# The last feed-forward layer of a four-layer model: one-hot tiles of 128 columns, additions between gathers, dense matmuls ahead of each search

## What is computed

```
logits = xf @ Wr + br                      # xf: 2048 x 128, 8 experts
Sm = softmax(logits, axis=-1)
G_t, idx_t = top_k(Sm.T, 256)              # per expert: its 256 tokens
G = G_t.T
idx = idx_t.T
tokens = xf[idx]
group = arange(8) // 2                     # two experts share W_up
mid = silu(einsum('keh,ehf->kef', tokens, W_up[group]) + b_up[group])
out = einsum('kef,efh->keh', mid, W_down) + b_down
y = zeros_like(xf).at[idx].add(G[..., None] * out)

x = x + tanh(g_ffn[3]) * y                 # with xf = layernorm(x)
```

## Time and profile before

| | us |
|---|---|
| median of 3 runs | 2270.3 |
| their lowest and highest | 2265.45, 2286.44 |
| the profiled execution | 2255.81 |
| its span in the trace | 2254.0 |
| mean granted TensorE clock, share of 2.4 GHz | 0.908 |

### The profile page before, as it was taken

One profiled execution on the slowest core, in us unless ns is written; L12 is line 12 of the kernel. 1 busy time (PEld: TensorE's weight loads), 2 busy tenths in 40 slices (PEclk: granted clock), 3 DMA queues, 4 the chain that ended last, 5 costly groups with the idle time before them and its releaser, 6 DMA issues. The chain is left out here.

```text
span 2254.0 us, 42793 instructions
## 1 busy us (share of the span) xinstructions
PE 1914.4 (85%) x16881; PEld 1121.5 (50%) x16881; DVE 1295.5 (57%) x2286; ACT 980.9 (44%) x1888; POOL 908.1 (40%) x1216
## 2 busy tenths in 40 slices
PE   6888887669999999957939999999978969999434
PEld 2333334446666666645724666666655524444423
DVE  4988893156565665524436655555522268886471
ACT  1554453216445545424524555555432317666101
POOL 2587750006556556523034666656540021110024
PEclk9999997759999999988968999999995989999557
DMA  6311100200000000022020000000000021210202
GB/s 216 118 49 37 36 11 0 73 13 9 2 5 5 5 1 2 2 91 69 23 75 5 5 5 5 5 1 2 1 12 2 1 66 45 58 54 15 79 17 22
DMA packets 78710, 69.97 MB, mean 31 GB/s; under 512 B 11744, under 2 KB 68209, under 8 KB 78485
## 3 DMA queue, kind: packets, MB, share of 16 engines
q1 hardware_dynamic: 71789, 53.12, 8.4%
q10 hardware_dynamic: 2888, 9.97, 1.1%
q0 software_dynamic: 3840, 4.20, 1.0%
HBM read 50.47 MB, written 17.31 MB: 30 GB/s over the span
## 5 line engine op out<-in xcount | busy, mean ns | idle before, releaser
L759 POOL TENSOR_TENSOR L1x_fold<-L1x_probs 128x512 f32<-128x512 f32 x128 | 162.6, 1270 | 171.3 <-ACT L1x_probs L827 166.5
L759 POOL TENSOR_TENSOR L2x_fold<-L2x_probs 128x512 f32<-128x512 f32 x128 | 162.7, 1271 | 161.3 <-ACT L2x_probs L827 156.5
L827 ACT ACTIVATE L1x_probs<-L1x_st_ps 128x512 f32<-128x512 f32 x256 | 139.0, 594 | 144.5 <-PE L1x_st_ps L969 143.5
L358 ACT ACTIVATE L0x_probs<-L0x_st_ps 128x512 f32<-128x512 f32 x256 | 139.1, 596 | 138.9 <-PE L0x_st_ps L431 122.2
L827 ACT ACTIVATE L2x_probs<-L2x_st_ps 128x512 f32<-128x512 f32 x256 | 139.0, 594 | 138.9 <-PE L2x_st_ps L969 138.9
L1131 DVE TENSOR_REDUCE L2x_neg_max<-L2x_row_ps 128x2 f32<-128x1024 f32 x128 | 156.3, 1221 | 49.0 <-PE L2x_row_ps L955 49.0
L1131 DVE TENSOR_REDUCE L1x_neg_max<-L1x_row_ps 128x2 f32<-128x1016 f32 x128 | 155.2, 1212 | 48.2 <-PE L1x_row_ps L955 48.1
L546 DVE TENSOR_REDUCE L3x_neg_max<-L3x_row_ps 128x2 f32<-128x1024 f32 x128 | 156.5, 1223 | 28.5 <-PE L3x_row_ps L420 26.2
L358 ACT ACTIVATE L3x_probs<-L3x_st_ps 128x512 f32<-128x512 f32 x256 | 139.1, 595 | 73.3 <-PE L3x_st_ps L431 73.1
L546 DVE TENSOR_REDUCE L0x_neg_max<-L0x_row_ps 128x2 f32<-128x1024 f32 x128 | 155.0, 1214 | 8.3 <-PE L0x_row_ps L420 7.4
L987 PE MATMUL L2x_u_ps<-L2x_probs,L2x_vst 128*64 128x256 f32 x1024 | 124.6, 385 | 1.2 <-ACT L2x_probs L827 1.2
(11 more groups left out here) (589 smaller groups left out, 4863.5 us busy)
## 6 DMA issues: line engine op xcount, KB each, us to landing
L0w_up<-in_L_ffn_up_weights ACTq DMA_DIRECT2D x9, 512.0 KB
L0w_down<-in_L_ffn_down_weights ACTq DMA_DIRECT2D x9, 512.0 KB
L0x_kst<-scratch_L0x_k SPq DMA_DIRECT2D x8, 512.0 KB, 4.0
L3x_kst<-scratch_L3x_k SPq DMA_DIRECT2D x8, 512.0 KB, 4.2
scratch_L0x_k<-L0x_k_hi SPq DMA_DIRECT2D x16, 128.0 KB, 2.4
L0x_qst<-scratch_L0x_q SPq DMA_DIRECT2D x8, 256.0 KB, 2.8
scratch_L3x_k<-L3x_k_hi SPq DMA_DIRECT2D x16, 128.0 KB, 2.4
L3x_qst<-scratch_L3x_q SPq DMA_DIRECT2D x8, 256.0 KB, 2.8
```

Source lines behind the costliest of these rows:

```text
L358: act.activation(probs[n % PROBS][:, 2 * half:2 * half + 2, :], st_ps[half][:, :, :], ACT.Exp, scale=sh.scale).then_inc(exp_ready, 1)
L759: pool.tensor_tensor(fold[:, :, :], pr[:, 0:2, :], pr[:, 2:4, :], ALU.add).then_inc(fold_step, 1)
L827: act.activation(probs[:, (2 * n + hh) % 8, 2 * half:2 * half + 2, :], st_ps[fill % 2][:, :, :], ACT.Exp, scale=sh.scale).then_inc(exp_rea ...
```

## The change

In the router block the bias no longer comes by matmul: `br` is loaded to all partitions, TensorE issues 16 logical matmuls in place of 32, and VectorE adds the bias before the maximum. At the end of that block `second` marks tokens with a place above 128, and `pos_T` becomes the place within its half, 1 to 128. In the expert block GpSimd first writes `halves`: `facts` twice, masked for either half. `pick` compares 128 columns in place of 256, and `find` takes 16 matmuls with six moving columns in place of 32 with three. Six matmuls over a constant tile (`keep_busy`) stand ahead of each `find`. `down` starts with the bias and waits for each part of `mid` by itself. ScalarE has one tiny SiLU at the start of the block. The orders of calls change on TensorE, VectorE and GpSimd. The diff, cut to its core:

```
-        wr, br = sb("wr", [P, experts]), sb("br", [1, experts])
+        wr, br = sb("wr", [P, experts]), sb("br", [P, experts])
...
-                        pe.matmul(logits[:, t, :], xnT[:, t * P:(t + 1) * P], wr[:, :], start=True, stop=False)
-                        ins = pe.matmul(logits[:, t, :], ones[0:1, 0:P], br[:, :], start=False, stop=True)
+                        ins = pe.matmul(logits[:, t, :], xnT[:, t * P:(t + 1) * P], wr[:, :], start=True, stop=True)
...
+                    dve.tensor_tensor(e[:, :, :], logits[:, :, :], br[:, :].unsqueeze(1).broadcast_to([P, NT, experts]), ALU.add)\
+                       .then_inc(biased, 1)
+                    dve.wait_ge(biased, 1)
...
-                    dve.tensor_scalar(pos_T[:, :, :], back_ps[:, :].rearrange("p (t e) -> p t e", e=experts), 1.0, None,
-                                      ALU.subtract)
+                    dve.tensor_scalar(second[:, :, :], place, P + 0.5, None, ALU.is_gt).then_inc(late, 1)
+                    dve.wait_ge(late, 2)
+                    dve.scalar_tensor_tensor(pos_T[:, :, :], second[:, :, :], -float(P), place, ALU.mult, ALU.add)
...
-            picks = [sb2(f"picks{i}", [P, NT, chosen], F16) for i in range(3)]
+            picks = [sb2(f"picks{i}", [P, NT, P], F16) for i in range(3)]
...
+                    pool.tensor_tensor(halves[:, :, :, 1, :], facts[:, :, :, :],
+                                       second[:, :, :].unsqueeze(3).broadcast_to([P, NT, experts, 3]), ALU.mult).then_inc(halves_ready, 1)
+                    pool.wait_ge(halves_ready, 1)
+                    pool.tensor_tensor(halves[:, :, :, 0, :], facts[:, :, :, :], halves[:, :, :, 1, :], ALU.subtract)\
+                        .then_inc(halves_ready, 1)
...
-                    for e in range(experts):
+                    for e in range(5):
                         gather(e)
                     pool.wait_ge(out_stored, 16)
-                    for e in range(experts):
+                    add_up(0)
+                    for e in range(5, experts):
+                        gather(e)
+                        add_up(e - 4)
+                    for e in range(4, experts):
                         add_up(e)
...
+                    def keep_busy(count):
+                        for _ in range(count):
+                            pe.matmul(idle_ps[:, :], dense[:, 0:P], dense[:, :], start=True, stop=True)
+
                     def find(e):
+                        keep_busy(6)
...
+                        if e == 0:
+                            pe.wait_ge(halves_ready, 2)
+                        for t in range(NT):
+                            ins = pe.matmul(facts_ps[e % 2][:, :, :].rearrange("p i n -> p (i n)"), picks[e % 3][:, t, :],
+                                            halves[:, t, e, :, :].rearrange("p i n -> p (i n)"), start=(t == 0), stop=(t == NT - 1))
...
+                            pe.matmul(y_ps[k % 2][:, :], ones[0:1, 0:P], bd[0:1, e, :], start=True, stop=False)
                             for c, (_, n) in enumerate(spans):
+                                if q == 0:
+                                    pe.wait_ge(mid_ready, 3 * g + c + 1)
...
                     def weigh(g):
-                        if g == 0:
-                            dve.wait_ge(tokens_ready, experts)
+                        dve.wait_ge(tokens_ready, 2 * g + 2)
```

More of the change, by code:

```diff
@@ L2252, in choice_ffn @@
             mid = [[sb2(f"mid{i}_{c}", [P, 512]) for c in range(3)] for i in range(2)]
-            facts_ps = [ps(f"facts{i}", [P, 2, 3]) for i in range(2)]
+            facts_ps, idle_ps = [ps(f"facts{i}", [P, 2, 3]) for i in range(2)], ps("idle", [P, SK])
             xT_ps, y_ps = ps("xT_ps", [P, 4, P]), [ps(f"y{i}", [P, D]) for i in range(2)]
@@ L2293, in find @@
                             pe.wait_ge(tokens_ready, e - 1)
-                        for i in range(2):
-                            for t in range(NT):
-                                ins = pe.matmul(facts_ps[e % 2][:, i, :], picks[e % 3][:, t, i * P:(i + 1) * P], facts[:, t, e, :],
-                                                start=(t == 0), stop=(t == NT - 1))
+                        if e == 0:
[3 more added lines that the diff above has]
+                                            halves[:, t, e, :, :].rearrange("p i n -> p (i n)"), start=(t == 0), stop=(t == NT - 1))
                         ins.then_inc(facts_ready, 1)
@@ L2326, in down @@
                                 pe.wait_ge(ys_ready, k - 1)
+                            pe.matmul(y_ps[k % 2][:, :], ones[0:1, 0:P], bd[0:1, e, :], start=True, stop=False)
                             for c, (_, n) in enumerate(spans):
-                                pe.matmul(y_ps[k % 2][:, :], mid[g % 2][c][0:n, q * P:(q + 1) * P], wd[0:n, e, c, :],
-                                          start=(c == 0), stop=False)
-                            pe.matmul(y_ps[k % 2][:, :], ones[0:1, 0:P], bd[0:1, e, :], start=False, stop=True).then_inc(y_ready, 1)
-                    for e in range(4):
+                                if q == 0:
+                                    pe.wait_ge(mid_ready, 3 * g + c + 1)
+                                ins = pe.matmul(y_ps[k % 2][:, :], mid[g % 2][c][0:n, q * P:(q + 1) * P], wd[0:n, e, c, :],
+                                                start=False, stop=(c == 2))
+                            ins.then_inc(y_ready, 1)
+                    for e in range(5):
                         find(e)
                     turn(0)
-                    find(4)
+                    find(5)
                     up(0)
-                    find(5)
+                    find(6)
+                    down(0)
                     turn(1)
-                    find(6)
+                    find(7)
                     up(1)
-                    find(7)
-                    down(0)
+                    down(1)
                     turn(2)
-                    down(1)
                     up(2)
+                    down(2)
                     turn(3)
-                    down(2)
                     up(3)
@@ L2368, in _ @@
                     act.wait_ge(wd_loaded, 16 * 7)
+                    act.activation(warm[:, :], ones[0:1, 0:1], ACT.Silu)
                     upper(0)
```

37 lines of the change are left out of this document (21 added, 16 removed).

## The result

| | kernel before | changed kernel |
|---|---|---|
| median, us (19 runs each) | 2276.48 | 2262.35 |
| lowest and highest | 2265.45, 2299.46 | 2243.98, 2274.32 |
| the profiled execution | 2255.81 | 2256.59 |
| its span in the trace | 2254.0 | 2254.8 |
| mean granted clock | 0.908 | 0.904 |

The ratio of the runs is 0.9934, 95% interval 0.9911 to 0.9957: by this ratio it is faster by 15.0 us of 2276.5 (10 to 20), so clear of zero and still within the 1% that counts as no change here. The profiled execution of the kernel before, 2255.81, was faster than each of its 19 runs.

The account below looks back on a forecast made before the run. GpSimd's serial chain of additions was taken as the bound, which can only be started earlier. Terms: -8.4 + 0.7 before the expert block, -9.2 within it, +1.5 in the chain, so -15.4 us: 2254.9 us, range 2241 to 2272.

Parts of the forecast that it names:

- Logits: Last sublayer's logits on TensorE: with 16 matmuls left, eight fast and eight slow, 8.4 us go.
- Bias and places: End of the router block: added VectorE instructions for bias, second and pos_T cost 0.7 us, all on the path.
- One-hot tiles: VectorE's comparisons in the expert block: 0.158 us each in place of 0.196, a pick 2.55 in place of 3.14.
- `halves`: Two GpSimd instructions of 1.0 us each, charged whole, 2.0 us, to pick(0) as holding up VectorE; bounds 0 to 3.0.
- To the first addition: Expert block from its start to GpSimd's first addition: 28.9 us in place of 38.1.
- the rival in which it falls and rises in turn: TensorE's clock falls and rises within the search; price between the forecast and the half-clock rival; no chance of its own.
- signs of being wrong: An addition waiting for a ys, a find ending later than its pick plus 0.6 us, or time outside 2241 to 2272.
- The chain: GpSimd's serial additions: three gathers between them add 0.5 us each, 1.5 in all; 0 at best, 7.8 at worst.
- The order alone: GpSimd's order in the expert block: with additions still behind all gathers, the first addition comes some 7 us later.
- Half clock: Rival, chance 0.07: TensorE stays at half clock in the expert block, +8 us in sum, 2278 on the median.

Follow-up runs that it names:

- e4_bias_alone: The kernel before with only the bias moved from TensorE to VectorE; last sublayer 138.41 us against 149.06 before.
- e5_full_tiles: The changed kernel with 256-column one-hot tiles, 32 matmuls in a find and no halves; last sublayer 134.55 us against 131.48.
- e3_halves_on_vector: The changed kernel with the two halves instructions moved from GpSimd to VectorE, behind pos_T; last sublayer 131.32 us against 131.48.
- e2_gathers_first: The changed kernel with GpSimd's old order, all eight gathers and then all additions; last sublayer 136.35 us against 131.48.
- v2_up_first: The changed kernel with up(0), down(0) and weigh(0) earlier, dense matmuls ahead of the first five finds only; median 2258.37 us, ratio 0.9904 to before.
- v4_turn_first_no_dense: v3_turn_first without any dense matmul; last sublayer 134.26 us against 125.80.
- e6_old_order: The changed kernel with the old orders of calls on TensorE and VectorE, GpSimd keeping the new one; last sublayer 137.46 us against 131.48.
- e1_no_dense: The changed kernel without the six constant matmuls ahead of each find; last sublayer 133.13 us against 131.48.
- v5_dense_in_gaps: v3_turn_first with dense matmuls also in TensorE's idle time around turn(0); median 2268.94 us, ratio 0.9922 to before; last sublayer 126.70 us.
- v3_turn_first: v2_up_first with turn(0) ahead of find(4), which has no dense matmuls; median 2255.93 us, ratio 0.9895 to before; last sublayer 125.80 us.

## Why the prediction was right, and where it was not

The forecast was 2254.9 us with a saving of 15.4. The runs gave a saving of 15.0 by the ratio, from a median that was itself 6 us higher than the one shown, and so 2262.35, inside the range and within 1% as given most chance. That 15.0 lies so near to 15.4 is luck, as its interval is 10 to 20; the sublayer itself saved 17.6. By its steps:

- *Logits*, -8.4 forecast, -10.3 measured, just past my bound of -10.1; it is the term that was most mis-sized. The clock fell when I said it would, 2.5 us in. What failed is "With 16 matmuls left, eight go fast again and eight slow": eleven went fast, since I kept the distance of the mixed sequence (0.157 a pass) for one that no longer alternates (0.112, and 0.214 for 0.26 at half clock). e4_bias_alone shows it by itself.
- *Bias and places*, +0.7 forecast, +0.64 measured.
- *One-hot tiles*. From 2191.45 it is 2.60 us to the start of the instruction behind 16 comparisons: 0.163 each, where I had 0.158 from 38 ns saved. The Trainium skill, "VectorE: DVE Perf Modes", section "The perf-mode tier table", gave an estimated 33 ns saved, so 0.163; the trace agrees with the page. The cleanest pair says the same: with no work of GpSimd's beside them, the first 32 comparisons took 6.36 us in e5_full_tiles and 5.29 in e3_halves_on_vector, 33 ns less each. (The groups, 25.9 and 22.9 us, also hold the hold-up of the next point.) `keep`, taken at 0.24, costs 0.14 from start to start (2194.05 to 2194.18).
- *`halves`*, 2.0 charged for two instructions of 1.0; they took 0.86 each, and by e3_halves_on_vector they held DVE up by 1.25, not for their whole length. That DVE is slowed while GpSimd computes is shown; that it stands still is not.
- *To the first addition*, 28.9 forecast, 29.41 measured, but partly by misses that cancel: 0.75 less hold-up and 0.3 less for three `keep`s on one side; on the other the comparisons, 0.3 more, and `up(0)`, which took 3.29 us and not 2.3, with its first six matmuls at half clock. I had PE at full clock from the second `find` on. It rose only at about 2184, behind the third, and fell once again, behind the 2.71 us and not behind the two gaps of 0.73 us ahead of `find(3)` and `find(4)`; the rival in which it falls and rises in turn had so much of it. One of my own signs of being wrong showed as well: `find(1)` ended at 2181.74, 1.0 us behind its `pick` (2174.16 + 6.54) and not 0.6, because its six constant matmuls ran at half clock. It cost nothing, since `keep(1)` comes behind `pick(2)`.
- *The chain*, +1.5 forecast, +0.69 measured. A gather costs a step 0.5, as I took it (6.40 to 6.45 by 5.90). But in the kernel before the first two steps were 6.12 and 6.74 already, so it had less to lose; and the bound was not the DMA with a gather hidden behind it but GpSimd itself, busy throughout.
- *The order alone*, "the first addition some 7 us later": 6.58 by e2_gathers_first.
- *Half clock*, given 0.07 and +8 us. The point from which it decides held up: where `down(1)` ran at 0.50 the third expert's addition waited for its `ys` (a step of 10.0 in v2_up_first and v4_turn_first_no_dense, of 7.70 in e6_old_order), and in no other kernel. What failed is the price, "groups 1 to 3 lose 5.3 each" and "+7.3". In the forecast's own order e1_no_dense lost 1.8 us to the first addition and nothing behind it; v4_turn_first_no_dense lost 4.0 and 4.4, since the clock came back with the end of `up(2)`. I had let it stay down to the end. (These runs leave the dense matmuls out. Dense matmuls that themselves run at half clock to the end, which the rival also took in, were not seen.)

What stays open: why the granted clock falls where it does. In the changed kernel it fell in PE's idle time of 2.71 us. In e2_gathers_first and e3_halves_on_vector PE idled for the same 2.71 us at the same place, and `up(0)` ran at full clock. In v2_up_first it fell at about 2200, inside `down(0)`, with PE busy. Dense matmuls in the gap (v5_dense_in_gaps) kept it up through `up(0)`, but then it was down in `up(1)`. No run separates what PE did before from when it did it, so the 1.7 and 8.5 us that the dense matmuls were worth hold for these traces. The 17.6 us are not taken apart to the end either: the two orders and the dense matmuls were only taken away one at a time, and what each is worth in that way does not add up to the whole.

## What to carry to other kernels

Take the distance of instructions from a sequence of the very same kind: a price that is read in a mixed sequence carries the cost of the mixing, and removing one kind also cheapens the other. Before pricing a slower clock or a later result, ask what slack the waiting chain leaves: the same dense matmuls were worth 1.7 us in one order and 8.5 in another. And when a change touches the last twentieth of a kernel, compare from a mark where it begins, since here the unchanged rest drifted by 38 us while the stretches of the changed part repeated to 0.2. And before an experiment's loss is put down to its edit, look whether several engines stopped at once where none had anything to wait for.

## What the runs showed of the hardware that I had not expected

- PE was busy without a gap for 14.8 us of e1_no_dense (2196.00 to 2210.80) and the granted clock stood at 0.50 all through; it read 0.97 only from 2215. In v2_up_first it was at 0.50 from about 2200 to 2227, with PE busy for 23.3 of the 26.5 us from 2200.50. In v3_turn_first it was back at full clock 3.2 us after it fell.
- One-row matmuls that alternate with 128-row ones cost 0.045 us more a pass at either clock, so that removing half of the passes took away 68% of the time.
- Two GpSimd instructions of 0.86 us slowed 16-bit comparisons on DVE by 1.25 us in all. GpSimd's issues of gathers and additions, of 0.95 to 1.65 us, slowed them hardly: from the first of 16 comparisons to the instruction behind them it was 2.59 to 2.68 us, beside such issues or not.
- A step of additions that waits for nothing else is 5.8 to 6.0 us, in every kernel here: two issues of 1.56, a gap of 0.30 and 2.5 us of waiting for the DMAs. None of it is time of the other engines.
